# Two attention layers written out one after the other, with semaphores of their own, and the second's Wq loaded from the first's last block

## What is computed

```
x = layernorm(x + gnn0(x))                      # layer0
for l in range(2):                              # layer1, the part that is changed
    q = (x @ Wq[l].T + bq[l]) * scaling; k = x @ Wk[l].T; v = x @ Wv[l].T
    scores = q[tgt] . k[src] per head; w = softmax of scores over the edges of one tgt
    agg = segment_sum(w * v[src], tgt)
    x = batchnorm(x + agg @ Wo[l].T + bo[l])
    x = batchnorm(x + relu(x @ W1[l].T + b1[l]) @ W2[l].T + b2[l])
x = layernorm(x + layernorm(x, ln_g, ln_b))     # and so on: layer2, the edge messages, a wide network
```

## Time and profile before

| | us |
|---|---|
| median of 3 runs | 3116.82 |
| the 3 runs | 3118.02, 3116.82, 3109.52 |
| the profiled execution | 3094.92 |
| its span in the trace | 3092.7 |
| TensorE clock granted, mean | 0.954 of full speed |
| attention layer, pass one (902.4 to 1442.5 in the span) | 540.1 |
| attention layer, pass two (1442.5 to 1985.0) | 542.5 |

### The profile page before, as it was taken

The page is one execution under the profiler, slowest core; times in us unless marked ns, Lnnn a source line. Parts: engine busy times, 40 slices in busy tenths (PEclk is TensorE's granted clock), DMA queues, the critical chain, the costliest instruction groups (busy, mean ns, idle before and its releaser), DMA issues. The chain is left out here.

```text
span 3092.7 us, 51722 instructions
## 1 busy us (share of the span) xinstructions
PE 2757.2 (89%) x13929; PEld 2139.9 (69%) x13929; DVE 2280.9 (74%) x4694; ACT 1864.5 (60%) x4322; POOL 1096.0 (35%) x1121
## 2 busy tenths in 40 slices
PE   7999999999879999986999999596999999988688
PEld 4588885555448888863888886355676777667576
DVE  8699989999853788854378885555788888776576
ACT  2599998888222666731267673142777777763560
POOL 1000000000530666742066674415666666630221
PEclk9999999999989999997999999798999999989899
DMA  2300000000434454422444545414777778860201
GB/s 71 102 0 0 0 0 0 0 0 0 141 121 162 120 141 136 131 76 77 162 120 142 135 130 75 115 43 158 234 244 245 245 244 245 228 166 1 99 1 41
DMA packets 121359, 336.32 MB, mean 109 GB/s; under 512 B 20103, under 2 KB 34378, under 8 KB 121230
## 3 DMA queue, kind: packets, MB, share of 16 engines
q0 software_dynamic: 55648, 172.54, 19.3%
q1 hardware_dynamic: 65582, 162.17, 17.4%
HBM read 242.16 MB, written 84.61 MB: 106 GB/s over the span
## 5 line engine op out<-in xcount | busy, mean ns | idle before, releaser
L1819 POOL DMA_INDIRECT x_got<-table_dram,src_idx x376 | 380.6, 1012 | 231.6 <-DVE msg L1949 135.4
L742 POOL DMA_INDIRECT feature_rows<-in_edge_attr,ids x376 | 367.8, 978 | 117.4 <-issue 111.5
L745 POOL COPY ids<-id_idx 128x136 uint32 (+2 forms) x5 | 1.2, 241 | 1089.6 <-DVE id_idx L860 782.2
L1949 DVE TENSOR_TENSOR msg<-bank,x_got 128x512 f32<-128x512 f32 x376 | 253.0, 684 | 140.2 <-PE bank L1844 106.3
L548 PE MATMUL bank<-row_hot,col_part 125*128 125x432 f32 x1600 | 327.9, 367 | 3.5 <-ACT col_part L612 3.5
L548 PEld LDWEIGHTS bank<-row_hot,col_part 125*128 125x128 f32 x1600 | 288.0, 188 | 43.5 <-ACT col_part L612 33.5
L1293 DVE TENSOR_TENSOR pt_low<-bank,pt_high 128x640 fp32r<-128x640 f32 x320 | 250.3, 819 | 88.7 <-ACT pt_high L1257 74.3
L693 ACT ACTIVATE hot_rest<-hot_dst,slot_w 128x128 bf16<-128x128 bf16 x864 | 272.6, 399 | 37.6 <-DVE hot_dst L653 37.6
L1257 ACT CAST pt_high<-bank 128x640 fp32r<-128x640 f32 x320 | 208.3, 696 | 120.1 <-PE bank L1210 96.3
L1287 DVE CUSTOM_DVE_ANT_0 p<-bank,log_counts 128x1254 f32<-128x1254 f32 x160 | 232.8, 1455 | 24.2 <-PE bank L1194 16.3
L1898 ACT ACTIVATE msg_high<-msg 128x512 fp32r<-128x512 f32 x329 | 206.8, 629 | 65.1 <-DVE msg L1949 45.6
(11 more groups left out here) (409 smaller groups left out, 6950.9 us busy)
## 6 DMA issues: line engine op xcount, KB each, us to landing
features_dram<-feature_parts POOLq DMA_DIRECT2D x94, 512.0 KB
edge_got<-features_dram SPq DMA_DIRECT2D x94, 512.0 KB
qk_dram<-qk_high SPq DMA_DIRECT2D x16, 640.0 KB, 2.9
qk_dram<-qk_low SPq DMA_DIRECT2D x16, 640.0 KB, 4.2
keys<-qk_dram SPq DMA_DIRECT2D x32, 320.0 KB
queries<-qk_dram SPq DMA_DIRECT2D x32, 320.0 KB
queries_low<-qk_dram SPq DMA_DIRECT2D x32, 320.0 KB
acc_a<-zeros SPq DMA_DIRECT2D x1, 6400.0 KB, 29.6
```

The lines of the kernel that those rows point to most:

```text
L742: pool.indirect_dma_start(out=rows[:, g % 2, j * ED:(j + 1) * ED], out_offset=None, in_=self.a.edge_attr_128, in_offset=bass.IndirectOffse ...
L1819: pool.indirect_dma_start(out=xg[:, g % XRING, j, :], out_offset=None, in_=k.table_dram, in_offset=bass.IndirectOffsetOnAxis(ap=k.src_idx[ ...
L1949: dve.tensor_tensor(msg[:, j, :], k.bank[:, 2 + j, :], xg[:, r, j, :], ALU.add).then_inc(added_x, 1)
```

## The change

The loop becomes two copies of its body in the program, made by a Python loop. `layer_state` allocates 62 semaphores for each copy (their names end in _0 and _1), so nothing has to be cleared between them, and the block with the 62 clears is gone. The place and the load of Wq move out of `project` into this state, and `finish_layer` of the first copy gets the state of the second (`following`): its SP issues the second's Wq behind W1 and W2. `project` of the second copy no longer issues Wq. The region of `finish_layer` now ends where `wqkv_rows_a` begins; every tile keeps its address.

The semaphores of the three stages ahead are now cleared and freed between `layer0` and `layer1`, with one clearing instruction and a barrier; those of `Features` are allocated earlier and kept.

```
 def project(nc, k, a, l, at):
...
-    w_loaded, w_turned, w_high, w_low = [S(f"wqkv_loaded{j}") for j in range(3)], S("wqkv_turned"), S("wqkv_high"), S("wqkv_low")
+    w_loaded, w_turned, w_high, w_low = at.w_loaded, S("wqkv_turned"), S("wqkv_high"), S("wqkv_low")
...
-    rows_a, w_a = r.take("wqkv_rows_a", [P, KC, D], F32), r.take("wqkv_a", [P, 2, KC, D], F32R)
+    assert r_rows_a == at.wq_at
+    rows_a = at.wq_rows
+    w_a = Region(nc, at.wq_at + 4 * KC * D, k.tail - 4 * KC * NP).take("wqkv_a", [P, 2, KC, D], F32R)
...
         def _(sp):
-            def load(j):
-                sp.dma_start(rows[j][:], weights[j][bass.ds(l, 1), :, :].rearrange("l (o p) i -> p (l o) i", p=P)).then_inc(w_loaded[j], 16)
-
-            load(0)
-            load(1)
+            if l == 0:
+                at.load_w(sp, rows_a, 0)
+            at.load_w(sp, rows_b, 1)
...
             sp.wait_ge(w_turned, KC)
-            load(2)
+            at.load_w(sp, rows_a, 2)
...
-def finish_layer(nc, k, a, l, at, features):
+def finish_layer(nc, k, a, l, at, features, following):
...
-    r = Region(nc, at.wo_rows_end, k.tail - 4 * KC * NP)
+    r = Region(nc, at.wo_rows_end, at.wq_at)
...
             for j in (1, 2):
                 at.load_wo(sp, j)
+            if following:
+                following.load_w(sp, following.wq_rows, 0)
...
-def layer1(nc, k, a, features):
+def layer_state(nc, k, a, l):
 
     at = Names()
-    at.sems = []
 
     def sem(name):
-        at.sems.append(nc.alloc_semaphore(name))
-        return at.sems[-1]
-
-    at.sem = sem
+        return nc.alloc_semaphore(f"{name}_{l}")
+
+    at.sem, at.l = sem, l
...
-    with nc.Fori(0, LAYERS) as l:
-        at.l = l
+
+    at.wq_at = at.temps + 2 * 4 * 2 * NP + 2 * 4 * KC * NP
+    at.wq_rows = Region(nc, at.wq_at, k.tail - 4 * KC * NP).take("wqkv_rows_a", [P, KC, D], F32)
+    at.w_loaded = [sem(f"wqkv_loaded{j}") for j in range(3)]
+
+    def load_w(sp, rows, j):
+        w = (a.L1_gnn_Wq, a.L1_gnn_Wk, a.L1_gnn_Wv)[j]
+        sp.dma_start(rows[:], w[bass.ds(l, 1), :, :].rearrange("l (o p) i -> p (l o) i", p=P)).then_inc(at.w_loaded[j], 16)
+
+    at.load_w = load_w
+    return at
+
+
+def layer1(nc, k, a, features):
+
+    states = [layer_state(nc, k, a, l) for l in range(LAYERS)]
+    for l, at in enumerate(states):
         project(nc, k, a, l, at)
         attend(nc, k, a, l, at, features)
-        finish_layer(nc, k, a, l, at, features)
-        with nc.Block() as block:
-            @block.gpsimd
-            def _(pool):
-
-                for s in at.sems:
-                    pool.sem_clear(s)
+        finish_layer(nc, k, a, l, at, features, states[l + 1] if l + 1 < LAYERS else None)
...
     used = nc.snapshot_sems()
+    features = Features(nc, k, a)
+    used_by_edges = nc.snapshot_sems()
     sort_edges(nc, k, a)
     edge_matrices(nc, k)
-    features = Features(nc, k, a)
     layer0(nc, k, features)
+    nc.clear_and_free_semaphores(nc.allocated_since(used_by_edges))
+    nc.all_engine_barrier()
     layer1(nc, k, a, features)
```

More of the change, by code:

```diff
@@ L1 @@
+import collections
 import concourse.bass as bass
@@ L69 @@
 class Region:
+    times = collections.Counter()
     def __init__(self, nc, start, end):
@@ L78, in take @@
             size *= n
-        t = self.nc.alloc_sbuf_tensor_at(name, shape, dt, offset=self.at)
+        Region.times[name] += 1
+        again = f"_{Region.times[name]}" if Region.times[name] > 1 else ""
+        t = self.nc.alloc_sbuf_tensor_at(name + again, shape, dt, offset=self.at)
         self.at += -(-size // 32) * 32
@@ L960, in project @@
     x = (x_high, x_low)
-    weights = (a.L1_gnn_Wq, a.L1_gnn_Wk, a.L1_gnn_Wv)
     rows, w_in = (rows_a, rows_b, rows_a), (w_b, w_a, w_a)
@@ L2440, in program @@
 def program(nc, a, out):
+    Region.times.clear()
     k = Names()
```

## The result

The changed kernel takes 3093.85 us, the median of five runs (3093.85, 3098.17, 3090.33, 3092.34, 3099.35). The kernel before, run five times beside it, takes 3116.82 (3109.52 to 3118.49). The medians are 23.0 us apart. The ratio, which takes in all the runs, is 0.9936, its 95% interval 0.9917 to 0.9956: 20 us less, between 14 and 26. The direction was forecast, the size was not: 3103.7 was forecast, with a range of 3097 to 3111, and the median lies 3 us beneath that range.

What follows compares the result with a forecast made beforehand. PE is busy for 89% of the span, so time is lost mainly where PE stands still. Terms -10.1 - 4.3 + 1.3 = -13.1 us, taken from 3116.82, give 3103.7 us; range 3097 to 3111.

Steps and rivals of the forecast that it cites:

- the middle border: Between first and second layer: without clears, jump back and wait for Wq, the first product comes 10.1 us sooner.
- The chain on DVE: At a projection's start, DVE's low parts set the first product: second `px_low` 3.6 us, product 13.5 behind the barrier.
- the last border: Between the second layer's end and `layer2`: clears and loop exit go, 4.3 us less (bounds 4.0 and 4.4).
- the added border: Between `layer0` and `layer1`: new clearing and barrier cost 1.3 us more, at least 0.56 and at most 1.5.
- the costs of nothing: Wq's early load hides behind some 90 us of `finish_layer`; Wk, landing in 5.1 us, is in time: no cost.
- rival with a late Wk: Second copy's entry: Wk takes its old 8.7 us, lands 1.3 late; sum -11.1, 3105.7 us; chance 0.04.
- The rival with a fetch at the entry: Branch into the second copy costs a 3 us fetch, middle worth 7.1; sum -10.1, 3106.7 us; chance 0.07.
- PE, ACT and DVE have the same instructions: Whole program: the edits leave these three engines' instructions unchanged, listed among the edits at no cost.
- the gain given back: Stages behind the border lose 4 us or more as the granted clock's phase moves; 3108 to 3113 us; chance 0.11.
- slower by the clock: PE rests less, so stays at its lower clock 48 us longer, losing 22.5 us; 3127 us; chance 0.03.
- from the border to the time: Last step: the trace's 13.1 us carried whole to the median, 3116.82 - 13.1 = 3103.7 us, as border waits are alike.

Runs made afterwards that it cites:

- clears_back: The changed kernel with a block of 62 single semaphore clears put back behind each copy; 2991.75 us, ratio 0.9982 to the kernel before.
- early_in_loop: The kernel before, loop and 62 clears kept, with only Wq loaded early, the first in a small block ahead of the loop; 2997.38 us, ratio 0.9997.
- null: First repeat of both kernels, sources unchanged: the kernel before 2998.96 us (ratio 0.9999), the changed kernel 2983.41 us (0.9951).
- again: Second repeat of both kernels, sources unchanged: the kernel before 3001.45 us (ratio 1.0003), the changed kernel 2982.81 us (0.9948).
- third: Last repeat of both kernels, sources unchanged: the changed kernel 2980.95 us (ratio 0.9945), the kernel before 2999.30 us (1.0006).
- early_range_loop: The kernel before, loop kept, with Wq loaded early and each pass's 62 clears made one range clear and barrier; 3106.47 us, ratio 0.9976.
- null_before: The kernel before, unchanged, timed against itself; 2998.96 us against 2998.77, ratio 0.9999.
- after_again: The changed kernel, unchanged, timed again beside the kernel before; 2982.81 us, ratio 0.9948.

## Why the prediction missed

**Right: the middle border.** -10.1 forecast, -10.3 in the first pair of traces; from the end of `finish_layer` to the end of the second projection it is 116.9 to 117.9 us in four traces of the kernel before and 107.1 to 107.5 in four of the changed one, 10.1 apart in the mean. The chain on DVE was the right thing to follow: 3.5 and 13.4 us behind the barrier against 3.6 and 13.5. (The places that the prediction itself gives make 10.2 of it, not 10.1.)

**Right: the last border.** -4.3 forecast, -4.4 measured.

**Mis-sized: the added border.** 1.3 forecast, 0.9 measured (0.8 to 0.9 in all). The term took over the 739 ns of the clearing in the earlier trace rows; over fewer semaphores it took 377, as the lower bound allowed for.

**Right: the costs of nothing.** Wq was in place long before; the traffic behind the second copy's entry, Wk, ended at about 1446.8, 4.9 us after its issue, and 2.8 ahead of its first turn at 1449.58; at the same entry of `clears_back` the profile has 5.3 us from its issue to its landing (5.1 forecast). This answers the rival with a late Wk.

**The rival with a fetch at the entry** did not come about: 0.1 us from the barrier to the cast. A fetch there is, but it belongs to the jump back: 3.6 us and four pieces of instructions in `early_in_loop`. The Trainium skill (Runtime: NRT & Kernel Launch, Instruction fetch mechanics) has an engine wait for the target's page when a taken branch leads outside the window held; the traces agree, with 3.6 us behind the far jump and 0.1 at the entry of the next block. The prediction didn't say what the copies are worth by this: of the middle's 10 us, 3.7 are the missing jump once the load is early, and without the copies the early load and the range clear give 7.5 us together (2.5 to 12.5). Nor is it right that PE, ACT and DVE have the same instructions: each lost the loop's own, and on PE one of them was the jump, 3877 ns in the kernel before:

```profile
L1515 PEldq COMPARE_BRANCH  x2: 83/1980/3877, 1442.6 to 1985.2; - x2
```

This didn't harm the number, since the forecast took pass one, which has no jump ahead of it, as its model.

**Not borne out: the gain given back, and slower by the clock.** The lower level lasted no longer than in pass one, and on the chips of 2999 us the edge messages are as long as before within 1 us and the two attentions in sum within 3.

**The step that failed is the last one, from the border to the time**: "I take the difference over: 3116.82 - 13.1 = 3103.7", with a range that ended at "the largest gain with 4 us of the runs' spread". Its sum of -13.1 was right within 0.7 us. But it set the whole of the program outside the borders at a difference of nothing, with 4 us for the runs' spread. The runs show more. Outside the borders, measured to the end of the projection, the trace of before was longer than that of the changed kernel by -13.4, -1.4, 4.2 and 12.4 us in the four pairs (the first, `null`, `again`, `third`). The ratio of the first timing is known only to 6 us either way, and the profiled execution of before had already lain 15 to 23 us beneath its fellows (3094.92 against 3109.52 to 3118.02). That should have widened the range below. Of the 9.9 us between 3103.7 and 3093.85 the borders' sum explains 0.7. Three later timings of the same two kernels give 0.9951, 0.9948 and 0.9945, that is 14.7, 15.6 and 16.5 us: the borders' 13.8 with 1 to 3 us that no border shows, inside each interval. Some of these may be the shorter copies of `finish_layer`: three of the eight in the four changed traces took 86.3 to 89.9 us, while the other five and all eight passes of before took 91.5 to 92.2. That the change brings this about isn't shown, since `early_in_loop` and `early_range_loop` have such a pass too (89.4 and 86.4).

**Open.** Whether the change gained more than its borders on the first chip is not settled. Against it: `early_range_loop` on a chip of the same 3115 us gave 7.5 us, as its borders did (6.8 at the pass ends, 1.4 in the projection, less 0.8 for its small block: 7.4). That run's interval, 2.5 to 12.5 us, is wide. For it stands only the first timing, 14 to 26 us, whose lower end just holds the borders' value. The changed kernel wasn't run on such a chip again. What made the profiled execution of before so short isn't shown either.

## What to carry to other kernels

At a border where all engines wait, price each wait by taking it away together with the others: load, jump back and clears stand behind or beside one another, and here the range clear alone gave 4 us and the early load alone nothing that could be measured, while all of it gave 15. In this loop, whose body is fetched anew on each pass (23 and 25 blocks of instructions), the jump was paid in full as soon as the loads behind it were early; writing the body out twice removed that, and the early load was only worth its price then. Carry a difference of traces to a median with the spread of the ratio, not of one side; ask first how the profiled execution stands to its fellows, and how far two traces of one kernel differ where nothing was changed.

## What was not expected of the hardware

**Single clears against a range.** 62 single clears cost 4.2 to 4.9 us, one clear over a range 0.37 us for these 62 and 0.74 for all semaphores since the program's start.

**Chips differ by 4%.** The same kernel takes 3115 us on some and 2999 on others; the mean granted clock is 0.9505 and 0.953, too near to each other to account for it (see the last point). Two stages make the difference. Windows of the edge messages, the profile of before and then `null_before`:

```profile
2135.00:2769.00 634.00, 577.15 (x2632) 433.28 (x2632) 492.29 (x804) 478.12 (x1034) 380.63 (x376) 0.97 0.79 234
```

```profile
2120.00:2684.00 564.00, 547.07 (x2636) 438.94 (x2635) 495.83 (x812) 474.26 (x1035) 408.33 (x371) 0.98 0.84 263
```

The stage moves the same data at 234 GB/s on the one and 263 on the other. The attention takes 331.1 and 317.2 us in pass one; this group of ACT has idle time of "issue" on the first chip and none on the second (again before, then `null_before`):

```profile
L1257 ACT CAST pt_high<-bank 128x640 fp32r<-128x640 f32 x320 | 208.3, 696 | 120.1 <-PE bank L1210 96.3 <-issue 23.1
```

```profile
L1257 ACT CAST pt_high<-bank 128x640 fp32r<-128x640 f32 x320 | 206.5, 697 | 100.7 <-PE bank L1210 100.7
```

The cast lasts equally long; what is added is waiting. Its cause wasn't looked for. The borders, by contrast, are equal on both chips to 0.2 us, apart from the 0.7 us by which the start of a projection varies.

**The spread goes with the clock.** Of 17 runs of the kernel before beside `early_range_loop`, each with its mean granted clock, the time falls by 1.8 us per 0.001 of clock (correlation -0.66; 22 runs beside `after_again`: 2.3 us, -0.84). A thousandth of 3000 us is 6 us more at the lower level, which at 0.47 lost for each is an estimate of 2.8. So the spread between runs goes with how long the granted clock is at the lower level; which of the two is the cause isn't shown, since this time holds waits too. In the wait behind the jump of `early_in_loop` PE does nothing and the clock is at 0.50:

```profile
1429.10:1432.60 3.50, 0.00 (x0) 0.00 (x0) 0.00 (x0) 0.00 (x0) 0.00 (x0) 0.50 0.58 123
```

Taking 14 us of such waits out of 3000 lifts the mean clock by 0.0023, an estimate from this row; in the three later timings the changed kernel's mean clock was 0.0024 to 0.0027 above that of the kernel before. The higher mean is thus no gain of its own. The profiled execution of before had 0.954, those 17 runs 0.9505 in the mean: by the slope this goes with 6 us of its lead, not 20.
